# A two-layer Perceiver on one core: the loads and first products ordered anew at the begin, and the self-attention's head halves turned instead of folded

## What is computed

```python
q = _mh_rmsnorm((x @ Wq).reshape(b, n, QH, DH).transpose(0, 2, 1, 3), q_gamma)   # QH 16, DH 64
k = _mh_rmsnorm(k, k_gamma)                                                      # H 8 heads
q = q.reshape(b, H, g, n, DH)                                                    # g = QH // H = 2
sim = jnp.tanh(jnp.einsum('bhgid,bhjd->bhgij', q, k) / 50.0) * 50.0 * DH ** (-0.5)
attn = jax.nn.softmax(jnp.where(causal, neg, sim), axis=-1)
out = jnp.einsum('bhgij,bhjd->bhid', attn, v)                                    # summed over g
return out.transpose(0, 2, 1, 3).reshape(b, n, H * DH) @ Wout
```

## Time and profile before

| | |
|---|---|
| median of 3 runs | 1825.33 us (1823.52 to 1828.67) |
| the profiled execution | 1825.6 us, its span 1823.8 us |
| TensorE (PE) busy | 1768.4 us, 97% |
| VectorE (DVE) | 1341.2 us, 74% |
| ScalarE (ACT) | 1018.6 us, 56% |
| GpSimd (POOL) | 939.8 us, 52% |
| chain that ended last | TensorE 77%, VectorE 12%, ScalarE 4%, issue 3%, DMA 2% |
| x0 / sa / ff, about | 0 to 655 / 655 to 772 / 772 to 812 |

### The profile page before, as it was taken

How to read it: one execution, slowest core, us unless ns; L and a number is a source line. 1 busy time by engine, 2 the same in 40 slices (tenths; PEclk the granted TensorE clock), 3 DMA queues, 4 the chain that set the end, 5 groups by cost and what they waited for, 6 DMA issues and landing times.

```text
span 1823.8 us, 44768 instructions
## 1 busy us (share of the span) xinstructions
PE 1768.4 (97%) x17870; PEld 1542.8 (85%) x17870; DVE 1341.2 (74%) x2790; ACT 1018.6 (56%) x2139; POOL 939.8 (52%) x1180
## 2 busy tenths in 40 slices
PE   7999999999999999999999999999999999999998
PEld 6888888888887778899999999999999986668886
DVE  6888888888888877567776767676767655767775
ACT  5677676767667745454445445444444433536664
POOL 3787877777777617446433333343333302524553
PEclk9999999999999999999999999999999999999999
DMA  6121111121110110044222222222223107041111
GB/s 166 38 74 39 38 39 38 48 65 38 38 38 2 60 51 1 13 122 126 67 64 64 64 64 64 64 64 64 64 65 93 34 1 304 1 185 35 33 32 16
DMA packets 50750, 113.11 MB, mean 62 GB/s; under 512 B 4928, under 2 KB 37264, under 8 KB 49008
## 3 DMA queue, kind: packets, MB, share of 16 engines
q1 hardware_dynamic: 46128, 105.13, 19.5%
q0 software_dynamic: 4416, 5.12, 1.6%
HBM read 105.78 MB, written 5.37 MB: 61 GB/s over the span
## 4 chain that ended last, share of the span: by engine, by line
PE 77%; DVE 12%; ACT 4%; issue 3%; DMA 2%; POOL 1%; SPq 0%; POOLq 0%; DVEq 0%
PE ps L104 8%; PE ps L166 7%; PE ps L1782 5%; PE ps L514 5%; PE ps L495 5%; PE ps L472 4%; DVE arenaR L1903 3%; PE ps L2786 3%; DVE arena L1909 3%; PE ps L1783 3%; PE ps L489 3%; PE ps L424 2%; DMA wsb<-in_ctxT 2%; PE ps L1706 2%; PE ps L2760 2%
## 5 line engine op out<-in xcount | busy, mean ns | idle before, releaser
L617 DVE TENSOR_REDUCE arena<-ps 128x1 f32<-128x400 f32 (+1 forms) x512 | 258.1, 567 | 90.9 <-PE ps L472 90.5
L777 ACT ACTIVATE arena<-ps 128x384 f32<-128x384 f32 (+1 forms) x512 | 223.3, 524 | 95.0 <-PE ps L495 93.8
L1782 PE MATMUL ps<-arenaR 128*128 128x386 f32 x768 | 266.4, 392 | 0.0
L878 POOL TENSOR_TENSOR arena<-arena 128x512 f32<-128x512 f32 (+1 forms) x152 | 197.2, 1297 | 76.7 <-ACT arena L777 68.4
L2013 ACT CAST arenaR<-ps 128x512 fp32r<-128x512 f32 (+1 forms) x256 | 123.0, 507 | 184.3 <-PE ps L166 175.4
L1783 PE MATMUL ps<-arenaR 128*128 128x194 f32 x768 | 194.8, 254 | 0.0
L166 PE MATMUL ps<-ident,wsb 128*128 128x128 f32 (+1 forms) x832 | 160.0, 273 | 3.5 <-ACT wsb L2038 1.7
L2038 ACT ACTIVATE wsb<-ps,arena 128x1200 f32<-128x1200 f32 x64 | 80.9, 1264 | 131.8 <-DVE arena L1962 131.8
L1783 PEld LDWEIGHTS ps<-arenaR 128*128 128x128 f32 x768 | 146.8, 191 | 0.0
L1782 PEld LDWEIGHTS ps<-arenaR 128*128 128x128 f32 x768 | 145.5, 189 | 0.6 <-DVE arenaR L1903 0.5
L1903 DVE TENSOR_TENSOR arenaR<-ps,arenaR 128x512 fp32r<-128x512 f32 (+1 forms) x256 | 138.3, 582 | 3.9 <-ACT arenaR L2013 3.7
(11 more groups left out here) (390 smaller groups left out, 5094.3 us busy)
## 6 DMA issues: line engine op xcount, KB each, us to landing
wsb<-in_ctx SPq DMA_DIRECT2D x16, 1152.0 KB
wsb<-in_ctxT SPq DMA_DIRECT2D x16, 800.5 KB, 5.1
wsb<-in_ctxT SPq DMA_DIRECT2D x32, 400.2 KB, 7.3
gu<-in_m_gu SPq DMA_DIRECT2D x8, 1536.0 KB, 19.0
arena<-in_ctxT SPq DMA_DIRECT2D x15, 800.5 KB, 5.2
arena<-in_ctxT SPq DMA_DIRECT2D x30, 400.2 KB, 7.2
dn<-in_m_dn SPq DMA_DIRECT2D x8, 768.0 KB, 11.3
wsb<-in_f_w SPq DMA_DIRECT2D x2, 1024.0 KB, 5.9
```

The lines of the kernel that those rows point to most:

```text
L617: e.tensor_reduce(mx4[n % 2][:, u, i:i + 1], ps[:, at("look", n, i, u), 0:400 + (i == 3)], AX.X, ALU.max).then_inc(c.maxed.at((n, i, u)), 1)
L777: e.activation(v[:, u, 0:128 * GN[s]], ps[:, at("st", n, s, u), 0:128 * GN[s]], ACT.Exp).then_inc(c.exp_a.at((x0, n, s, u)), 1)
L878: e.tensor_tensor(sums_p[0:k], sums_p[0:k], v[0:k, :, 128 * t:128 * t + 128], ALU.add).then_inc(added_p.at((n, s)), 1)
L1782: e.matmul(o, PTh[:, t, :], v[:, t, 0:386], start=(t == 0), stop=False)
```

## The change

**Begin of x0.** The first x tile is loaded first, and x, wk and wv have a semaphore each. The first 400 context columns are issued by ScalarE's queue, in front of its table load; SP loads columns 400 to 799 next, and 800 on behind the constants. TensorE starts with ten 512-column products on a tile of ones. The key products of the first piece for both head groups are made together, in the order in which their operands come (`first_keys`), and do not wait for wv. The small orders of TensorE, VectorE and ScalarE are rearranged.

**End of x0.** For the last head pair TensorE sums groups 2 and 3 of the probabilities (`summed_by_pe`), VectorE only 0 and 1.

**sa.** `fold` is replaced by `turn_o`, eight turns into banks 3 and 4; ScalarE copies one half of the columns (`take_half`), VectorE adds the other half (`add_half`). `finish` waits for that add, and so does the part of `output` that writes bank 4. Scores are made before `finish`. Tile 7 is projected into banks 3 to 6 in three parts; tile 6's root is taken by GpSimd too, and tile 6's values and squares apart. GpSimd splits w1 and takes ff's first root before the root of tile 7, and all roots before w2 and the adds. VectorE's masks, moments and adds are interleaved anew.

**ff.** The up-projections' banks are shifted by one, two tiles are normalised in ff itself instead of one.

The diff, cut to its core, in three pieces. x0:

```diff
+    def summed_by_pe(n):
+
+        return 4 if n < N - 2 else 3 if n == N - 2 else 2
...
+    def load_first(e, k, rows, half):
+
+        e.dma_start(raw1[0][:, k], d["ctxT"][0, 0:128, k]).then_inc(rows.at("rows" if rows is not half else None, 16), 16)
+        e.dma_start(raw2[0][0:64, k], d["ctxT"][0, 128:192, k]).then_inc(half.at(None, 16), 16)
+        e.dma_start(raw2[0][64:128, k], d["ctxT"][0, 128:192, k]).then_inc(half.at((x0, 0), 16), 16)
...
+        e.dma_start(c.x[:, 0, :], x[:, 0, :]).then_inc(in_tile.at("x", 16), 16)
         for k in ("wk", "wv"):
...
+            e.dma_start(W[k], d["x0_" + k]).then_inc(in_w[k].at(k, 16), 16)
+        load_first(e, slice(400, 800), in_second, in_second)
...
+        load_first(e, slice(800, NK), in_rest, in_rest)
...
+        def first_keys():
+
+            H, L, h, l, m = wh["wk"], wl["wk"], c1h[0], c1l[0], c2[0]
+            k, o = columns(0)[0], [ps[:, take("k", n, 0), 0:400] for n in range(2)]
...
+            w.wait_ge(*w_hi("wk"))
+            w.wait_ge(*c.split_hi((x0, 0, 0, 1)))
+            for n in range(2):
+                e.matmul(o[n], H[:, 0, f[n]], h[:, k], start=True, stop=False)
+            w.wait_ge(*c.dv(("weight low", "wk")))
+            for n in range(2):
+                e.matmul(o[n], L[:, 0, f[n]], h[:, k], start=False, stop=False)
+            w.wait_ge(*c.dv(("first low rows", 0)))
+            for n in range(2):
+                e.matmul(o[n], H[:, 0, f[n]], l[:, k], start=False, stop=False)
+            w.wait_ge(*c.split_hi((x0, 0, 0)))
+            w.wait_ge(*c.dv(("first low", 0)))
+            for n in range(2):
+                e.matmul(o[n], H[:, 1, f[n]], m[:, k], start=False, stop=False)
+                e.matmul(o[n], L[:, 1, f[n]], m[:, k], start=False, stop=True).then_inc(k_made.at((n, 0)), 1)
...
+                    terms = [(128 if G0[s] + t < 12 else KL, probs(n, s)[:, :, 128 * t:128 * t + 128])
+                             for s in range(summed_by_pe(n), 4) for t in range(GN[s])]
...
-        keys(0, 0)
+        w.wait_ge(*padded("ones"))
+        for i in range(10):
+            e.matmul(ps[:, 7, 0:512], onesR, onesR.unsqueeze(1).broadcast_to([128, 4, 128]), start=True, stop=True)
+        first_keys()
+        vals(0, 0)
         turn_h(0)
-        keys(1, 0)
-        vals(0, 0)
+        keys(0, 1)
         queries(0)
-        keys(0, 1)
         vals(0, 1)
         keys(0, 2)
...
+        weight_low("wk")
         first_low(0)
+        weight_low("wv")
         norm_tile(c, e, w, "in", 0)
-        for i in range(1, 4):
-            first_low(i)
+        first_low(1)
+        first_low(2)
         queries(0)
+        first_low(3)
...
+        load_first(e, slice(0, 400), in_rows, in_half)
...
+        weight("wk")
         split(0, 0)
+        weight("wv")
         keys(0, 0)
+        split(0, 1)
+        keys(1, 0)
         take_h(0)
-        keys(1, 0)
-        for i in range(1, 4):
-            split(0, i)
+        split(0, 2)
+        split(0, 3)
```

sa on TensorE:

```diff
-        return 4 * (t % 2) + i
+        return 4 * (t % 2) + i if t < NT - 1 else 3 + i
...
-        return slice(0, 4) if part == 0 else slice(4, NT - 1)
+        return slice(0, 4) if part == 0 else slice(4, NT - 2)
...
+    def both_halves(v):
+        return v.rearrange("p k (b q) -> p b k q", b=2)
+
+    def turned_half(j):
+
+        return ps[:, 3:5, :].rearrange("p b (k j q) -> p b k j q", j=2, q=64)[:, :, :, j, :]
...
         def output(t):
-            for b in range(4, 8):
+            for b in range(5, 8):
...
+            for k, pair in enumerate(((4, 0), (6, 2), (5, 1), (7, 3), (0, 4), (2, 6), (1, 5), (3, 7))):
+                if k in (0, 2):
+                    w.wait_ge(*masked((t, k // 2)))
+                if k == 4:
+                    w.wait_ge(*emptied[4])
+                for b, h in enumerate(pair):
+                    u, i, n = h % 2, h // 2, slice(64 * b, 64 * b + 64)
+                    p = e.matmul(ps[:, 4 + 2 * b + h // 4, 128 * (h % 4):128 * (h % 4) + 65],
+                                 flat(E[t % 2][n, 8 * u + 2 * i:8 * u + 2 * i + 2, :]), vx[n, t, h, :], start=True, stop=True)
+                    if k == 7:
+                        p.then_inc(c.summed.at((sa, t)), 1)
...
-        def fold(t):
+        def turn_o(t):
             w.wait_ge(*c.o_norm((sa, t, 1)))
             w.wait_ge(*emptied[3])
-            w.wait_ge(*c.in_const("small"))
             for b in range(2):
                 for k in range(4):
-                    p = e.matmul(ps[:, 3, 128 * k + 64 * b:128 * k + 64 * b + 64], flat(o1[:, 8 * b + 2 * k:8 * b + 2 * k + 2, :]),
-                                 c.fold, start=True, stop=True)
+                    p = c.turn(e, ps[:, 3 + b, 128 * k:128 * k + 128], flat(o1[:, 8 * b + 2 * k:8 * b + 2 * k + 2, :]))
             p.then_inc(c.o_turned.at((sa, t)), 1)
-            emptied[3] = c.a_out((sa, t))
+            emptied[3] = emptied[4] = added(t)
...
-            w.wait_ge(*c.a_out((sa, t)))
+            w.wait_ge(*added(t))
...
+        project_last("kv", (2, 3))
         turn_q(0)
         turn_k(0)
-        project(NT - 1, (1,))
+        project_last("q1", (1,))
         scores(0)
+        project_last("q0", (0,))
+        turn_k(1)
         for t in range(1, NT + 2):
-            if t == 1:
-                turn_k(t)
+            if t < NT:
                 turn_q(t)
-            elif t < NT:
-                turn_q(t)
+            if 2 < t < NT:
                 turn_k(t)
             if t == NT:
                 then.pe(e, w, 0)
             if t <= NT:
                 output(t - 1)
+            if t < NT:
+                scores(t)
+            if t == 1:
+                turn_k(2)
             if t >= 2:
                 finish(t - 2)
-            if t < NT:
-                scores(t)
             if t <= NT:
-                fold(t - 1)
+                turn_o(t - 1)
```

sa on the other engines, and ff:

```diff
+        def add_half(t):
+            w.wait_ge(*first_half(t))
+            e.tensor_tensor(both_halves(oT), turned_half(1), both_halves(oT), ALU.add).then_inc(added.at(t), 1)
...
+        norms(1)
         w.wait_ge(*gamma("in"))
         take_q(0)
-        norms(1)
-        project(NT - 1)
-        mask(0)
+        squares(NT - 2)
+        project_rest()
+        for u in range(2):
+            mask(0, u)
         for t in range(1, NT + 2):
             then.dve(e, w, t)
             if t < NT:
                 take_q(t)
+            if t == 1:
+                project_q0()
+            if t >= 3:
+                weigh(t - 3)
+            if t == NT:
+                then.dve_last(e, w)
             if t <= NT:
                 output(t - 1)
+            if t < NT:
+                mask(t, 0)
             if t >= 2:
                 finish(t - 2)
             if t < NT:
-                mask(t)
-            if t == 1:
-                squares(NT - 1)
-            if t == NT:
-                then.dve_last(e, w)
+                mask(t, 1)
+            if t <= NT:
+                add_half(t - 1)
+            if t in (2, 3):
+                squares_last(t - 2)
+        weigh(NT - 1)
...
-            e.copy(flat(oT), ps[:, 3, :]).then_inc(c.a_out.at((sa, t)), 1)
+            e.copy(both_halves(oT), turned_half(0)).then_inc(first_half.at(t), 1)
...
-        for t in range(4, NT - 1):
+        for t in range(4, NT - 2):
             project(t)
+        values(NT - 2)
         norms(1)
+        squares(NT - 2)
+        values(NT - 1)
         take_k(0)
...
             if t < NT:
                 take_k(t)
+            if t == 1:
+                w.wait_ge(*qkv((NT - 1, "q0")))
+            then.act(e, w, t)
+            if t < NT:
                 scores(t)
+            if t == NT:
+                then.act_last(e, w)
+                e.activation(c.sd[:, 0:1], c.ident[:, 0:1], ACT.Gelu).then_inc(c.ac.at(), 1)
+            if t <= NT:
+                take_half(t - 1)
             if t == 1:
                 squares(NT - 1)
-            if t == NT:
-                e.activation(c.sd[:, 0:1], c.ident[:, 0:1], ACT.Gelu).then_inc(c.ac.at(), 1)
-                then.act_last(e, w)
...
+            w.wait_ge(*sq_sum(t if t < NT - 1 else (t, 1)))
...
         for t in range(NT):
             if t == NT - 1:
-                root_of_last()
+                w.wait_ge(*masked((1, 1)))
+                then.pool_split(e, w, "w1")
+                then.pool_root(e, w, 0)
+            if t >= NT - 2:
+                root_of(t)
             normalise(t)
         then.pool(e, w)
...
-        u, o, bank = slice(512 * half, 512 * half + 512), slice(128 * f, 128 * f + 128), 4 + n % 4
+        u, o, bank = slice(512 * half, 512 * half + 512), slice(128 * f, 128 * f + 128), 4 + (n + 1) % 4
...
-        for tile in {6: (0, 1), 7: (2, 3), 8: (4, 5), 9: (6,)}.get(t, ()):
+        for tile in {5: (0,), 6: (1,), 7: (2, 3), 8: (4,), 9: (5,)}.get(t, ()):
...
+        norm_tile(c, e, w, into, NT - 2)
...
+        for i in range(4):
```

(14 more changed lines are left out.)

127 lines of the change are left out of this document (64 added, 63 removed).

## The result

| | before | after |
|---|---|---|
| median of the runs, us | 1827.1 (1823.5 to 1829.4, 6 runs) | 1816.4 (1812.7 to 1817.1, 6 runs) |
| profiled execution: time, span, us | 1825.6, 1823.8 | 1816.9, 1815.1 |
| ratio after to before | | 0.9940, 95% interval 0.9925 to 0.9954 |

A forecast was written before the change was run, and what follows sets the result against it. The prediction took TensorE to bound the kernel, busy 46.5 of 47 us in the self-attention's tile loop. Savings of 1.6 + 1.0 + 9.2 + 1.6 = 13.4 us took 1825.6 to 1812.2, range 1808.0 to 1818.5.

The forecast's parts named there:

- Begin: Start of the first cross-attention: first score products near 17.9 instead of 19.42, 1.6 us saved, bounds -0.5 to 3.5.
- so I leave its landing at 14.45: Start of the first cross-attention: wq, still SP's twelfth load behind the same bytes, lands unchanged at 14.45.
- landing 2 us earlier: Start of the first cross-attention: upper bound, 3.5 us saved, if DMA rings run better from two queues.
- Seam: First cross-attention to self-attention: TensorE sums more, VectorE's adds go, projection at 655.59 comes 1.0 us earlier, bounds 0.4 and 1.2.
- The exchange on TensorE: Self-attention tile loop: eight fold products (2.10 us) become eight turns (0.95), 1.15 us saved a tile, 9.2 in all.
- Its cover is thin but it holds: Self-attention tile loop: VectorE's work with the add, about 6.6 of 7.3 us a tile, stays hidden.
- Part 6: GpSimd's roots, splits and bias adds, self-attention loop and after: results come before they are due, cost nothing.
- rival A: Self-attention tile loop: VectorE's add behind both masks binds, tiles take 8.0 instead of 7.3 us, 1817.8 us; chance 0.17.
- Its cover is 6 us: Up-projections: GpSimd's w2 split and bias adds end about 786, first down-projection at 792.54, so no cost.
- Part 5: Waits before the self-attention loop and in its first tiles: 1.1 of 2.7 us left, 1.6 saved, bounds 0 and 2.7.
- Rival B: Start of the first cross-attention: loads bound by bytes, nothing or less gained at 19.42, 1813.8 to 1815 us; chance 0.10.
- Rival C: Self-attention tile loop: TensorE falls to the lower clock level with 20 turns in a row, 1841 us; chance 0.03.

The follow-up runs named there:

- run with one queue: The changed kernel with ScalarE's three first loads issued by SP again, ahead of all others; ratio to the kernel before 0.9945.
- run with the seam alone: The kernel before with only the last head pair's extra sums moved from VectorE to TensorE at the end of x0; median 1825.1 us, ratio 0.9996.

## Why the prediction was right, and where it was off

- **Begin: mis-sized, 1.6 for 3.94, of which 3.1 stayed.** From the queries to the first scores the sum was right, 1.62 for 1.57. The step that failed is "so I leave its landing at 14.45": wq landed at 12.15, issued at the same time, behind the same bytes, and the queries started 2.32 us earlier. The run with one queue puts 1.8 us on the three issues; the bounds' "landing 2 us earlier" was this case. The reading that the queries stand at 14.63 because of the load was not shown either: TensorE was busy until then, and only the run with the seam alone has it waiting for wq. In the changed kernel VectorE's low parts and the keys end last, 0.16 us behind the load, and the waits for the low parts are also why the ten warm-up products are worth only 0.36. The stall of 0.83 at 96.5 was in nobody's sum.
- **Seam: right**, 1.0 for 0.94 in the changed kernel and 0.96 alone.
- **The exchange on TensorE: right in kind, 1.15 a tile for 1.35.** The turns took 0.87 instead of 0.95, and 0.49 of the 1.35 came from the new place of the block in TensorE's order, which the step did not price: it took 2.10 as the fold's cost wherever it stands. The exchange alone is worth 0.87.
- **"Its cover is thin but it holds": it held in the undisturbed tiles, not beside GpSimd.** Part 6, "Cost nothing", counted only when GpSimd's results are due and not what its long instructions do to VectorE's while they run. That was rival A's mechanism, seen in the earlier trace rows, priced for every tile and then given to a rival instead of to the tiles where GpSimd's long instructions would stand: one tile lost 1.4, and one 0.5 to a norm beside a multiply. Two lost 0.2 each to the sums of squares, VectorE's own work. The fall of the clock, 1.6, stood in one of four executions with the wait.
- **The up-projections: the step "Its cover is 6 us" failed.** w2's split ended long before it was due, and still cost 1.5 by standing beside the low parts of the gelus, the adds 1.0; with 0.3 that no run explains, 2.8 in all. The earlier trace rows had shown the same stretch of a mask beside a split.
- From the projection to the up-projections the sum had 9.2 + 1.6 = 10.8; it was 8.2. With the loop's 3.9 us of losses given back it would have been 12.1. Part 5's share of this was not measured apart.
- **Rival B: no**, wq landed earlier, not later. **Rival A** came true in one tile, not in all.
- **Rival C: no.** Twenty turns in a row (2.4 us of 7.1, L166 in the loop above) ran at a granted clock of 1.00:

```profile
731.00:738.00 7.00, 6.95 (x92) 6.36 (x92) 6.08 (x13) 3.51 (x6) 4.30 (x13) 1.00 0.00 0
738.00:745.00 7.00, 7.00 (x96) 6.34 (x94) 5.84 (x13) 3.52 (x6) 1.54 (x6) 1.00 0.02 4
```

The one fall in the loop stands behind a wait of 0.88 us, and not in the three other executions with the same wait and the same turns. The Trainium skill's rule on turns (TensorE: Matmul & The Clock Gate, Part 4: PE-mode transpose), by which the loop was at risk, made no difference here.

The errors have both signs: +2.3 at the begin, +1.6 in the tiles' spacing, against -3.9, -2.8, -0.8 (the stall) and 0.75 lost behind the down-projections, which is within what executions differ by there; the rest are tenths. That the time came out inside the range is partly luck: 3.9 us that the sum did not have made up for half of the 8 it lost.

## What to carry to other kernels

An instruction moved to an engine that is "free" has to be costed against its neighbour on the other engine too: here GpSimd's subtracts and adds on SBUF stretched VectorE's masks and low parts from 0.69 to as much as 1.79 us, so they belong beside VectorE's PSUM instructions, behind a signal from the last mask, not only ahead of a due date. Put first on an in-order engine what the bounding engine waits for; moving the queries' copy and the last output ahead of work that nobody awaits gave 1.9 us, more than either split's new place. And before adding warm-up work, ask what ends the wait behind it.

## What the runs showed of the hardware

- A VectorE add or multiply of two SBUF inputs of 512 columns takes 0.69 us, and up to 1.79 beside a long GpSimd instruction in the changed kernel; a norm of one SBUF input of 256 columns 0.40, beside GpSimd's multiply 1.21 and beside its split of w2 1.50. Copies and adds that read PSUM kept their 0.69 and 1.22 throughout (L1294, L1268). The Trainium skill (GPSIMD Engine Reference, 1. Specifications) names two cases of contention, two SBUF inputs and the 2-port modes; the trace agrees for the first; whether the norm is a case of the second no run shows.
- The fold's 8 products (16 records) held TensorE 2.10 us behind products of 64 x 64 and 1.73 behind products of 128 x 128.
- TensorE stood 0.73 to 0.85 us for nothing shown, at the same instruction in each of the ten profiled kernels with the ten warm-up products, and in none of the four without them, two of which had the rest of the new begin. Why ten instructions more at the start do this 90 us later is open; another number of them was not tried.
- The row of the granted clock read 1.00 over the first 9 us of the kernel without warm-up, while its products followed each other every 0.33 us, the lower level. Before the first rise the spacing tells the level, and the row does not. A later fall does show: 0.76 and 0.67 in the run with one queue, whose first keys stood 0.33 apart behind the ten products.
